# Two cross attentions re-ordered: a head pipeline carried across key blocks, paired score matmuls, an earlier block count

## Chip, cores and metric

One Trainium2 chip, one of its cores. The metric is the device time of one execution, in microseconds (us); the median of the runs shown counts. Engines are named as in the profile: PE is TensorE (PEld its weight loads), DVE is VectorE, ACT is ScalarE, POOL is GpSimd, SP is SyncE, which issues all the DMAs here.

## The reference, cut to what matters

Two layers act on x (256 tokens x 256): a cross attention, a self attention and a feed-forward part each. The change touches the two cross attentions only. ctx is 4096 x 192; the mask leaves out the same trailing keys for every query.

```python
# layer 0: 16 heads of 64, masked
q = xn @ Wq;  k, v = split(ctx @ Wkv)            # Wkv 192 x 2048
out = softmax(where(mask, q k^T / 8, -inf)) v    # per head
x = x + out @ Wo + bo
# layer 1: one head of 256, no mask
q, k, v = xn Wq + bq, ctx Wk + bk, ctx Wv + bv
x = x + softmax(q k^T) v
```

Everything is float32. The profile counts each float32 matmul as two instructions.

## The kernel before

`build` writes one program per engine; the order within an engine is the order of the code, and semaphores tie the engines together. Tokens are two tiles of 128 (t = 0, 1).

**Ahead of the loop.** SP loads x, the identity, the mask, Wq and Wkv (L393 to L403). DVE normalizes x (`layer_norm`), PE turns it (`turn_xn`), ACT scales it into xnT (L976). DVE finds in `find_blocks` which of the eight 512-key blocks hold a key (L1191, L1194). PE projects q with 32 matmul instructions (L471) and counts the blocks between the first 8 and the other 24 (L478). `find_range` on DVE (L1201 to L1210) makes `first` and `n_blocks` from the count, and signals `range_set`. SP then loads both into registers and issues the DMAs of the first block (`load_block`, L409 and L411). PE makes keys and values of head pairs 0 and 1 (`keys_and_values`, L492 to L497: four matmuls of 512 columns, of which the two with 64 rows lie in different halves of the array), and only then does the loop start.

**First attention.** The loop runs over `n_blocks` blocks (two here), and in it over head pairs p = 0 to 7, each with two tiles t. Per pair and tile:

- PE `scores(p, t)`, L527: two heads, 64 rows each, into banks 2s and 2s+1 of slot s.
- DVE `maxima`, L1245 to L1253: adds the mask in place, takes the negated maxima, and the running ones.
- ACT `exps`, L1002: `prob`, and `alpha` = exp(old maximum - new one), L1006.
- PE `turn`, L538: eight transposes of `prob` into banks 4 (head e = 0) and 5 (e = 1).
- ACT copies bank 4 to `probT` (`copy_pT`, L1014), DVE copies bank 5 (L1259).
- Per pair, PE `values(p)`: transposes alpha (L546) and multiplies probT with the values (L553). DVE `add_values` (L1264, L1267) scales `o_acc` and adds.

PE's order in a step p is scores(p, 0), turn(p-1, 1), values(p-2), scores(p, 1), turn(p, 0), keys_and_values(p+2). Pairs 6 and 7 have no keys_and_values left. After pair 7 the block ends with keys_and_values(0) for the next block, values(6), turn(7, 1), keys_and_values(1) for the next block, values(7); the last block does these too, for a block that does not exist. The slots for scores and for keys and values are the same four banks 0 to 3. SP loads the next block when keys_and_values(7) is done.

**After the loop.** DVE inverts the sums l (L1293, L1295). PE spreads 1/l over 64 partitions per head with 64 matmul instructions against the identity (L584). DVE scales `o_acc` pair by two (L1300), PE projects with Wo (L594, 32 instructions). The next stages follow (L602 on).

**Second attention.** 8 units u: 1024 keys and one tile each, UNITS = 8, t = u % 2. Before it PE makes q4 (L804) and its product with Wk and bk (`qk_a` with 128 rows, `qk_b` with 65: 64 channels and the bias, against a row of ones in `ctxT_b`; L810). Per unit PE does `scores4` (L825 with 128 rows, L826 with 65, for two halves of 512 keys), `turn4(u-1)` (L836), `values4(u-2)` (L847). DVE finds the maxima (L1544, L1547), copies one half of p4T, and adds; ACT does the exponentials (L1125) and copies the other half (L1135).

Of the kernel before, what the change touches and what calls it, by code (L numbers as in the profile page):

```python
# [63 lines left out]
def build(nc, a, out):  # L64
    with ExitStack() as ctx:
# [50 lines left out]
        alpha = region_u[:, 5248:7296].rearrange("p (m t e d) -> p m t e d", m=XP, t=TT, e=2)  # L116
        region_d = sb("region_d", [P, 8192])
# [68 lines left out]
        ctxT_b = region_d[0:CD - P + 1, S2:2 * S2]  # L186
# [3 lines left out]
        qk_b = part(region_g, 768, T)[0:CD - P + 1]  # L190
# [6 lines left out]
        nm4_run = sb("nm4_run", [P, TT])  # L197
        nm4_new = sb("nm4_new", [P, TT])
# [66 lines left out]
        l_scaled, run_kept = sem("l_scaled"), sem("run_kept")  # L265
        l_ready, recip_psum = sem("l_ready"), sem("recip_psum")
# [112 lines left out]

        def keep_first(act, nth, banks):  # L380
# [11 lines left out]
        def _(sp):  # L392
# [13 lines left out]
            n_blocks = sp.value_load(rng_i[0:1, 1:2], min_val=1, max_val=NBLK)  # L406
# [7 lines left out]
            load_block(within(first, NBLK - 1))  # L414
            sp.dma_start(rows[:, :], a["rows"].partition_broadcast(P)).then_inc(rows_in, 16)
# [26 lines left out]
            sp.dma_start(ctxT_b[0:CD - P], a["ctxT"][P:CD, 0:S2]).then_inc(ctxT_in, 16)  # L442
# [19 lines left out]
        def _(pe):  # L462
            pe.wait_ge(ident_in, 16)
            pe.wait_ge(consts_set, 2)
            turn_xn(pe, 1, (bank[0], bank[1]))
            pe.wait_ge(weights_in, 16)
            pe.wait_ge(xnT_ready, 2)
            for m in range(8):
# [6 lines left out]
                if m == 1:  # L475
                    pe.wait_ge(blocks_seen, 1)
                    for t in range(TT):
                        mm = nc.tensor.matmul(bank[2][0:1, 0:NBLK], lhsT=ones[:, 0:1], rhs=seen[:, t, :],  # L478
                                              start=t == 0, stop=t == TT - 1)
                    mm.then_inc(blocks_counted, 1)  # L480

            def slot_of(p, t):

                return t if p == XP - 1 else (p + t) % 2

            def keys_and_values(p):

                own, s = slice(p * P, (p + 1) * P), p % 2
# [13 lines left out]
            pe.wait_ge(ctx_landed, 48)  # L502
# [5 lines left out]
            pe.wait_ge(q_ready, 4)  # L508
            with pe.Fori(0, n_blocks) as i:
# [5 lines left out]
                def scores(p, t):  # L515
                    s = slot_of(p, t)
                    pe.wait_ge(k_ready, base8 + (p + 1))
                    if p == XP - 1:
                        pe.wait_ge(prob_ready, base32 + (4 * (p - 1) + 2 * t + 2))
                    elif t == 1 or p == 0:  # L520
                        pe.wait_ge(k_ready, base8 + (p + t + 1))
                        pe.wait_ge(v_ready, base8 + (p + t + 1))
                    else:
                        pe.wait_ge(prob_ready, base32 + 4 * p)
# [6 lines left out]
                def turn(p, t):  # L531
                    u = 2 * p + t
                    for e in range(2):
                        pe.wait_ge(prob_ready, base32 + (2 * u + e + 1))
                        if u >= 1:
                            pe.wait_ge((pT_even, pT_odd)[e], base16 + u)
                        for k in range(KT_PER):
                            mm = nc.tensor.transpose(bank[4 + e][:, k * P:(k + 1) * P],  # L538
                                                     prob[:, u % 2, e, k * P:(k + 1) * P], ident[:, :])
                        mm.then_inc(pT_psum, 1)  # L540

                def values(p):
                    pe.wait_ge(o_added, base8 + (p + 1))
                    pe.wait_ge(alpha_ready, base16 + (2 * p + 2))
                    for t in range(TT):
# [1221 lines left out]
```

## Time and profile before

| | us |
|---|---|
| three runs | 519.38, 523.21, 525.88 |
| median | 523.21 |
| the profiled execution, its own time | 523.5 |
| its span (first to last instruction) | 521.7 |
| busy: PE | 465.3 |
| busy: DVE | 286.6 |
| busy: ACT | 171.2 |

The profile is that of the third line. Its span is 1.8 us shorter than that execution's time. Times in the rows count from the start of the span. A busy time is a union: two matmuls that run side by side count once.

### The profile page before, as it was taken

Reading aid. Unit: us, or ns where it says so; the run is one execution under the profiler, and the core shown is the slowest. Engines: PE = TensorE matmul, PEld = TensorE weight load, DVE = VectorE, ACT = ScalarE, POOL = GpSimd, SP = SyncE. Lnnn points to the kernel's source line nnn. Section 1 sums busy time; section 2 is a strip of 40 time slices with the busy share of each in tenths; the row PEclk is TensorE's granted clock in tenths of the full one; section 3 lists DMA queues with packets and bytes.
Section 4 is the critical chain, followed back from the end, with each engine's and each line's share of the span. In section 5 each row is a group of like instructions: output and inputs, shape, how many; then the busy total and the mean of one; then the engine's idle time right before and its main releaser. Section 6 shows DMA issues by size and latency. Waiting matters only on the chain.

```text
span 521.7 us, 8539 instructions
## 1 busy us (share of the span) xinstructions
PE 465.3 (89%) x3199; PEld 325.7 (62%) x3199; DVE 286.6 (55%) x925; ACT 171.2 (33%) x428; POOL 4.1 (1%) x6
## 2 busy tenths in 40 slices
PE   3888999878999889977769989989979999889997
PEld 2534554443545459874456878878855668767774
DVE  5155777455767644457746997960045444445332
ACT  1154555434555511364731232000013233124110
POOL 0000000000000000000000002000000000000000
PEclk9898999889999999998888999659999999989999
DMA  8300001000002910800004945600048000000000
GB/s 293 105 2 1 1 0 42 1 0 0 0 0 61 363 64 1 322 2 1 1 1 142 336 143 188 136 0 0 1 132 318 1 1 0 1 0 2 0 1 21
DMA packets 21469, 35.02 MB, mean 67 GB/s; under 512 B 1663, under 2 KB 18048, under 8 KB 20864
## 3 DMA queue, kind: packets, MB, share of 16 engines
q1 hardware_dynamic: 21440, 34.64, 20.5%
q8 instruction: 18, 0.29, 0.2%
q14 instruction: 11, 0.09, 0.1%
HBM read 34.37 MB, written 0.26 MB: 66 GB/s over the span
## 4 chain that ended last, share of the span: by engine, by line
PE 73%; DVE 16%; issue 5%; ACT 2%; DMA 1%; DVEq 0%; SPq 0%; POOL 0%; ACTq 0%
PE bank L553 6%; PE bank L538 6%; PE bank L793 6%; PE bank L931 5%; PE bank L527 4%; PE bank L495 4%; PE bank L847 3%; PE bank L492 3%; PE bank L493 3%; PE bank L825 3%; PE bank L826 3%; PE bank L783 2%; PE bank L471 2%; PE bank L945 1%; DMA region_a<-in_Wq 1%
## 5 line engine op out<-in xcount | busy, mean ns | idle before, releaser
L1002 ACT ACTIVATE region_g<-bank,nm_new 128x512 f32<-128x512 f32 x64 | 43.4, 683 | 59.8 <-DVE nm_new L1250 59.8
L538 PEld LDWEIGHTS bank<-ident,region_g 128*128 128x128 f32 x256 | 28.8, 145 | 36.3 <-ACT region_d L1014 24.4
L538 PE MATMUL bank<-ident,region_g 128*128 128x128 f32 x256 | 36.9, 289 | 12.1 <-ACT region_d L1014 7.4
L1245 DVE CUSTOM_DVE_ANT_0 bank<-bank,bias_h 128x512 f32<-128x512 f32 x64 | 43.0, 713 | 4.5 <-issue 4.5
L527 PE MATMUL bank<-region_a,qT 64*128 64x512 f32 x128 | 34.6, 619 | 0.0
L1221 DVE COPY region_a<-bank 128x512 f32<-128x512 f32 x18 | 12.5, 692 | 38.3 <-PE bank L497 38.3
L553 PE MATMUL bank<-region_d,region_a 128*64 128x256 f32 x256 | 32.8, 400 | 0.0
L793 PE MATMUL bank<-region_u,region_g 128*128 128x256 f32 x128 | 29.6, 396 | 1.5 <-issue 1.5
L318 ACT ACTIVATE root<-var 128x2 f32<-128x2 f32 x6 | 1.2, 203 | 87.7 <-DVE var L328 87.7
L783 PE MATMUL bank<-region_a 64*128 64x32 bf16 x768 | 27.3, 249 | 2.4 <-DVE region_a L1499 1.8
L793 PEld LDWEIGHTS bank<-region_u,region_g 128*128 128x128 f32 x128 | 25.5, 200 | 5.3 <-issue 1.6
L783 PEld LDWEIGHTS bank<-region_a 64*128 64x128 bf16 x768 | 26.2, 153 | 3.8 <-DVE region_a L1499 2.6
L762 PE MATMUL bank<-xnT,region_d 128*128 128x256 f32 x128 | 28.0, 379 | 0.0
L762 PEld LDWEIGHTS bank<-xnT,region_d 128*128 128x128 f32 x128 | 24.3, 190 | 3.7 <-issue 0.5
L931 PE MATMUL bank<-xnT,region_u 128*128 128x256 f32 (+1 forms) x112 | 25.6, 384 | 0.0
L1259 DVE COPY region_d<-bank 128x512 f32<-128x512 f32 x32 | 22.1, 692 | 5.7 <-PE bank L538 5.4
L553 PEld LDWEIGHTS bank<-region_d,region_a 128*64 128x64 f32 x256 | 17.5, 141 | 10.3 <-issue 3.6
L323 DVE BATCH_NORM_STATS2 bn<-bank 128x6 f32<-128x256 f32 x8 | 3.0, 422 | 37.8 <-PE bank L793 29.7
L931 PEld LDWEIGHTS bank<-xnT,region_u 128*128 128x128 f32 (+1 forms) x112 | 20.4, 186 | 4.6 <-issue 1.7
L492 PE MATMUL bank<-ctx_a,region_a 128*128 128x512 f32 x36 | 20.7, 661 | 2.0 <-issue 2.0
L847 PE MATMUL bank<-region_a,region_g 128*128 128x192 f32 x128 | 22.0, 326 | 0.0
L1125 ACT ACTIVATE region_g<-bank,nm_new 128x512 f32<-128x512 f32 x16 | 10.9, 683 | 33.8 <-DVE nm_new L1547 33.8
(299 smaller groups left out, 833.9 us busy)
## 6 DMA issues: line engine op xcount, KB each, us to landing
region_d<-in_downT SPq DMA_DIRECT2D x2, 2048.0 KB, 10.6
region_u<-in_up SPq DMA_DIRECT2D x2, 2048.0 KB, 11.9
region_a<-in_ctx SPq DMA_DIRECT2D x1, 3072.0 KB, 16.5
region_d<-in_w_q SPq DMA_DIRECT2D x1, 2048.0 KB, 12.3
region_d<-in_ctxT SPq DMA_DIRECT2D x1, 2048.0 KB, 11.5
region_u<-in_wg SPq DMA_DIRECT2D x1, 1728.0 KB, 7.8
region_u<-in_wu SPq DMA_DIRECT2D x1, 1728.0 KB, 11.7
region_a<-in_wd SPq DMA_DIRECT2D x1, 1664.0 KB, 15.9
```

What stands on the lines that cost most here:

```text
L492: nc.tensor.matmul(bank[2 * s][:, :], lhsT=wkv[:, 0, own], rhs=ctx_a[:, :], start=True, stop=False)
L527: mm = nc.tensor.matmul(bank[2 * s + e][:, :], lhsT=qT[own, p, t * P:(t + 1) * P], rhs=keys[own, p, :], start=True, stop=True)
L538: mm = nc.tensor.transpose(bank[4 + e][:, k * P:(k + 1) * P], prob[:, u % 2, e, k * P:(k + 1) * P], ident[:, :])
L553: mm = nc.tensor.matmul(bank[6 + p % 2][64 * e:64 * e + 64, 0:T], lhsT=v_blk[:, k, (2 * p + e) * XD:(2 * p + e + 1) * XD], rhs=probT[:, p ...
L762: mm = nc.tensor.matmul(bank[(6, 7, 0, 1)[b % 4]][:, (e % 2) * T:(e % 2 + 1) * T], lhsT=downT[:, c, e * P:(e + 1) * P], rhs=xnT[:, c, :], ...
L783: mm = nc.tensor.matmul(bank[2 + 2 * g + t][:, :].rearrange("p (h s) -> p h s", h=ET)[:, :, s], lhsT=hot_lo[own, g, :, s], rhs=hot_hi[own, ...
L793: mm = nc.tensor.matmul(bank[6 + t][:, 0:D], lhsT=hidden[:, e, t * P:(t + 1) * P], rhs=up[:, e, :], start=False, stop=e == ET - 1)
L847: mm = nc.tensor.matmul(bank[6 + u % 2][:, 0:CD], lhsT=p4T[:, u % 2, k * P:(k + 1) * P], rhs=ctx_rows[:, i * 8 + k, :], start=k == 0, stop ...
L931: mm = nc.tensor.matmul(bank[b][0:size, at:at + T], lhsT=w[:, c, m * P:m * P + size], rhs=xnT[:, c, :], start=c == 0, stop=c == DC - 1)
L1002: nc.scalar.activation(prob[:, u % 2, e, :], bank[2 * s + e][:, :], ACT.Exp, scale=-1.0, bias=nm_new[:, p, t, e:e + 1], accum_out=l_blk[:, ...
L1245: ins = nc.vector.tensor_tensor_reduce(bank[2 * s + e][:, :], bank[2 * s + e][:, :], bias_h[:, t, :], -1.0, 3e38, ALU.add, ALU.min, accum_ ...
L1259: nc.vector.tensor_copy(probT[:, p % 2, 1, :, t * P:(t + 1) * P], bank[5][:, :].rearrange("p (k q) -> p k q", k=KT_PER)).then_inc(pT_odd, 1)
```

## The change

1. **Count first.** On PE, 14 transposes of the identity into bank 3 (nothing reads them) and the block count stand ahead of the q projection. SP loads only `first` before the first block's DMAs; `n_blocks` and a new 128 KB load, `pick_pair`, come after them.
2. **Pipeline across blocks.** keys_and_values(0) and (1) move into the loop's start; values(6), turn(7, 1) and values(7) of a block run in the first steps of the next one, and after the loop for the last block. In the first block these slots work on zeroed buffers: four memsets on POOL at the start (prob 1024 elements a partition, alpha 512, probT 4096, v_blk 1024). No keys or values are made for a block that does not exist.
3. **Order and engines within.** For tiles t = 1 ACT copies both halves of probT (`turned_half`), ahead of exps(p+1, 0) but behind exps(7, 0) in step 7; for t = 0 ACT copies head e = 0 and DVE head e = 1, as before. In step 7, values(5) stands ahead of turn(6, 1). The sums l are added per pair in DVE's loop (`add_sums`) and no longer once a block.
4. **1/l.** Two transposes of `l_rep` and eight matmuls with 32 rows (`pick_pair`) in place of the 64 instructions; `scale_output` works per pair, pair 7 after values(7).
5. **Second attention.** The bias term leaves `qk_b`: its 64 rows are stored once per tile at partitions 64t, `ctxT_b` is loaded twice (two DMAs of 1 MB), and the 64-row matmuls of t = 0 and t = 1 follow each other for the same half. The bias is a column `q_bk4` (8 one-column instructions); `maxima4` adds one small DVE instruction, `shift4`. Two units form an iteration: turn4 and the 128-row scores of each tile, the four 64-row matmuls, then both values4.

The core of the diff (SP's, POOL's and allocation lines are told above):

```diff
             turn_xn(pe, 1, (bank[0], bank[1]))
+            for k in range(14):
+                nc.tensor.transpose(bank[3][:, k % 4 * P:(k % 4 + 1) * P], ident[:, :], ident[:, :])
+            pe.wait_ge(blocks_seen, 1)
...
+                pe.wait_ge(ctx_landed, base48 + 48)
+                keys_and_values(0)
+                turn(-1, 1, base16, base32)
+                keys_and_values(1)
                 for p in range(XP):
                     scores(p, 0)
+                    if p == XP - 1:
+                        values(p - 2, base8, base16)
                     if p >= 1:
-                        turn(p - 1, 1)
-                    if p >= 2:
-                        values(p - 2)
+                        turn(p - 1, 1, base16, base32)
+                    if p < XP - 1:
+                        values(p - 2, base8, base16)
                     scores(p, 1)
-                    turn(p, 0)
+                    turn(p, 0, base16, base32)
                     if p + 2 < XP:
-                        pe.wait_ge(prob_ready, base32 + (4 * p + 2))
                         keys_and_values(p + 2)
-                pe.wait_ge(ctx_landed, base48 + 96)
-                pe.wait_ge(prob_ready, base32 + 30)
-                keys_and_values(0)
-                values(XP - 2)
-                turn(XP - 1, 1)
-                pe.wait_ge(prob_ready, base32 + 32)
-                keys_and_values(1)
-                values(XP - 1)
-
+            values(-2, n_blocks * 8, n_blocks * 16)
+            turn(-1, 1, n_blocks * 16, n_blocks * 32)
             pe.wait_ge(l_ready, 1)
...
+            values(-1, n_blocks * 8, n_blocks * 16)
             pe.wait_ge(wo_in, 16)
...
+            for i in range(1, UNITS // TT + 1):
+                for t in range(TT):
+                    turn4(TT * (i - 1) + t)
+                    if i < UNITS // TT:
+                        scores4_a(i, t)
+                if i < UNITS // TT:
+                    for half in range(2):
+                        for t in range(TT):
+                            mm = scores4_b(i, half, t)
+                            if half == 1:
+                                mm.then_inc(s4_psum, 1)
+                for t in range(TT):
+                    values4(TT * (i - 1) + t)
...
+                copy_keys(0)
+                for e in range(2):
+                    turned_half(-1, 1, e, base32)
+                copy_keys(1)
                 for p in range(XP):
-                    exps(p, 0)
+                    if p == XP - 1:
+                        exps(p, 0)
                     if p >= 1:
-                        copy_pT(p - 1, 1)
+                        for e in range(2):
+                            turned_half(p - 1, 1, e, base32)
+                    if p < XP - 1:
+                        exps(p, 0)
                     exps(p, 1)
-                    copy_pT(p, 0)
+                    turned_half(p, 0, 0, base32)
```

## Rows read from the trace of the kernel before

**Rows 1.** Windows: length, busy us (instructions) of PE, PEld, DVE, ACT, POOL, granted clock, DMA, GB/s.
```profile
22.30:110.70 88.40, 82.62 (x418) 40.99 (x418) 51.61 (x156) 42.29 (x108) 0.00 (x0) 0.94 0.03 8
110.70:189.90 79.20, 72.81 (x402) 37.95 (x400) 51.17 (x156) 39.84 (x105) 0.00 (x0) 0.98 0.24 80
189.90:202.60 12.70, 10.86 (x100) 9.90 (x99) 4.84 (x11) 0.00 (x0) 0.00 (x0) 1.00 0.01 1
...
390.40:436.00 45.60, 45.59 (x192) 30.12 (x193) 20.70 (x58) 13.88 (x42) 0.00 (x0) 1.00 0.27 99
...
48.00:84.00 36.00, 36.00 (x204) 18.74 (x204) 25.11 (x77) 19.34 (x53) 0.00 (x0) 1.00 0.00 1
```

**Rows 2.** Timeline of PE, one step of the first attention: start, length, engine, instruction.
```profile
133.12 1.13 PE L527 MATMUL bank<-region_a,qT 64*128 64x512 f32 x4
134.18 1.09 PE L538 MATMUL bank<-ident,region_g 128*128 128x128 f32 x8
135.11 1.02 PE L492 MATMUL bank<-ctx_a,region_a 128*128 128x512 f32 x2
...
137.89 1.03 PE L527 MATMUL bank<-region_a,qT 64*128 64x512 f32 x4
...
140.09 1.95 PE L553 MATMUL bank<-region_d,region_a 128*64 128x256 f32 x16
141.96 1.13 PE L527 MATMUL bank<-region_a,qT 64*128 64x512 f32 x4
```

**Rows 3.** Timeline of PE around the loop's seams and behind it, with idle time before.
```profile
42.87 1.89 PE L538 MATMUL bank<-ident,region_g 128*128 128x128 f32 x8 [1.86 <-ACT region_d L1014]
...
115.35 1.97 PE L538 MATMUL bank<-ident,region_g 128*128 128x128 f32 x8 [2.68 <-ACT region_g L1002]
...
173.56 1.09 PE L538 MATMUL bank<-ident,region_g 128*128 128x128 f32 x8 [1.86 <-ACT region_d L1014]
...
195.38 7.17 PE L594 MATMUL bank<-wo,region_g 128*128 128x256 f32 x32
```

**Rows 4.** Timeline ahead of the loop, PE and SP's queue.
```profile
10.18 3.78 PE L471 MATMUL bank<-xnT,region_a 128*128 128x256 f32 x8 [2.68 <-DMA region_a<-in_Wq]
...
14.07 6.23 PE L471 MATMUL bank<-xnT,region_a 128*128 128x256 f32 x24
...
17.12 0.36 SPq L409 DMA_DIRECT2D ctx_a<-in_ctxT  x1
...
22.30 1.83 PE L492 MATMUL bank<-ctx_a,region_a 128*128 128x512 f32 x2 [1.99 <-issue]
```

**Rows 5.** Groups by line over the whole span: busy us, mean ns, idle before.
```profile
L1014 ACT COPY region_d<-bank 128x512 f32<-128x512 f32 x32 | 18.6, 581 | 4.5 <-PE bank L538 4.5
...
L355 PE MATMUL bank<-ident 128*128 128x128 f32 x104 | 13.3, 289 | 0.0
...
L584 PE MATMUL bank<-ident,l_blk 128*64 128x128 f32 x64 | 3.7, 274 | 1.8 <-DVE l_blk L1295 1.8
...
L635 PE MATMUL bank<-region_a 32*128 32x256 f32 x64 | 4.6, 400 | 1.0 <-DVE region_g L1359 1.0
...
L826 PE MATMUL bank<-region_d,region_g 65*128 65x512 f32 x32 | 16.4, 592 | 0.0
```

**Rows 6.** Timeline of ACT in the step of rows 2.
```profile
140.68 0.69 ACT L1002 ACTIVATE region_g<-bank,nm_new 128x512 f32<-128x512 f32 x1 [1.99 <-DVE nm_new L1250]
```

**Rows 7.** Timeline of the second attention: one unit of PE, and its last.
```profile
412.07 1.02 PE L825 MATMUL bank<-region_d,region_g 128*128 128x512 f32 x2
...
418.99 1.02 PE L825 MATMUL bank<-region_d,region_g 128*128 128x512 f32 x2
...
429.61 1.29 DVE L1544 TENSOR_REDUCE nm_half<-bank 128x1 f32<-128x512 f32 x2 [2.77 <-PE bank L826]
...
441.17 5.37 PE L847 MATMUL bank<-region_a,region_g 128*128 128x192 f32 x32
```

**Rows 8.** POOL's one large fill (groups by line), and DVE at the start (timeline).
```profile
L1693 POOL MEMSET region_d<- 1x4096 f32 x1 | 3.6, 3556 | 88.9 <-PE bank L762 88.9
...
4.62 0.17 DVE L328 TENSOR_SCALAR var<-mv 128x2 f32<-128x2 f32 x1
```

More of the change, by code:

```diff
@@ L474, in _ @@
                     mm.then_inc(q_psum, 1)
[L475 to L484, printed above, removed]
             def keys_and_values(p):
-                own, s = slice(p * P, (p + 1) * P), p % 2
+                own, s = slice(p * P, (p + 1) * P), slot_of("kv", p)
                 half, k = p // KT_PER, p % KT_PER
@@ L589, in _ @@
+            for j in range(2):
+                for g in range(4):
+                    own = slice(32 * g, 32 * g + 32)
+                    mm = nc.tensor.matmul(bank[g][:, j * T:(j + 1) * T], lhsT=pick_pair[own, j, :], rhs=l_T[own, :],
+                                          start=True, stop=True)
+            mm.then_inc(recip_psum, 1)
+            values(-1, n_blocks * 8, n_blocks * 16)
             pe.wait_ge(wo_in, 16)
             for c in range(8):
-                if c % 2 == 0:
-                    pe.wait_ge(oT_ready, c // 2 + 1)
+                pe.wait_ge(oT_ready, c + 1)
@@ L807, in _ @@
             pe.wait_ge(q4_ready, 2)
-            for m, rows_m in ((0, P), (1, CD - P + 1)):
+            for c in range(DC):
+                mm = nc.tensor.matmul(bank[3][:, 0:T], lhsT=wk4T[:, c, 0:P], rhs=q4T[:, c, :],
+                                      start=c == 0, stop=c == DC - 1)
+            mm.then_inc(qk4_psum, 1)
+            for c in range(DC):
+                for t in range(TT):
+                    mm = nc.tensor.matmul(bank[4][64 * t:64 * t + 64, 0:P], lhsT=wk4T[:, c, P:CD],
+                                          rhs=q4T[:, c, t * P:(t + 1) * P], start=c == 0, stop=c == DC - 1)
@@ L809, in _ @@
+            mm.then_inc(qk4_psum, 1)
+            for t in range(TT):
                 for c in range(DC):
-                    mm = nc.tensor.matmul(bank[3 + m][0:rows_m, 0:T], lhsT=wk4T[:, c, m * P:m * P + rows_m],
-                                          rhs=q4T[:, c, :], start=c == 0, stop=c == DC - 1)
-                mm.then_inc(qk4_psum, 1)
-            pe.wait_ge(ctxT_in, 32)
+                    mm = nc.tensor.matmul(bank[5][:, t:t + 1], lhsT=q4T[:, c, t * P:(t + 1) * P],
+                                          rhs=wk4T[:, c, CD:CD + 1], start=c == 0, stop=c == DC - 1)
@@ new lines, in scores4_a, with scores4_b @@
+            def scores4_a(i, t):
+                if i >= 1:
+                    pe.wait_ge(p4_ready, 2 * (TT * (i - 1) + t + 1))
+                for half in range(2):
+                    nc.tensor.matmul(bank[2 * t + half][:, :], lhsT=qk_a[:, t * P:(t + 1) * P],
+                                     rhs=ctxT_a[:, keys4(i, half)], start=True, stop=False)
+            def scores4_b(i, half, t):
+                own = slice(64 * t, 64 * t + 64)
+                return nc.tensor.matmul(bank[2 * t + half][:, :], lhsT=qk_b[own, :], rhs=ctxT_b[own, keys4(i, half)],
+                                        start=False, stop=True)
@@ L1303, in _ @@
+            dve.wait_ge(o_added, n_blocks * XP + 3)
+            for p in range(XP - 1):
+                scale_output(p)
+            add_values(-1, n_blocks * 8)
+            dve.wait_ge(o_added, n_blocks * XP + 4)
+            scale_output(XP - 1)
             dve.wait_ge(rows_in, 16)
```

304 lines of the change are left out of this document (161 added, 143 removed).

## The prediction

> **What bounds the kernel now.** I read the windows by stage first. In the two blocks of the first attention PE is busy 82.6 of 88.4 us and 72.8 of 79.2 us, DVE and ACT never over two thirds; in the second attention PE is busy throughout [rows 1]. So both stages are PE's, and time comes only from PE's work, its idle time or its clock. Then PE's timeline: a full step of the first attention lasts 8.84 us (133.12 to 141.96), of which keys_and_values is 2.78 (135.11 to 137.89); without it a step is 6.06 [rows 2]. From 48 to 84 us nothing but such steps runs, at clock 1.00 and with no gap [rows 1]. A block's work is therefore 6 x 8.84 + 2 x 6.06 + 2 x 2.78 = 70.7 us, and two blocks are 141.4.
>
> Last the seams. PE starts the first keys at 22.30 [rows 4] and the Wo projection at 195.38 [rows 3]: 173.1 us. Work explains 141.4 + 2 x 2.78 (keys made ahead of the loop, while the last block makes two pairs for nobody) + 3.7 for 1/l [rows 5] = 150.7. The other 22.4 us are idle time and low clock. Of these (1 - 0.94) x 88.4 + (1 - 0.98) x 79.2 = 6.9 us are clock [rows 1]: after the waits at 42.87 and 115.35 eight transposes take 1.89 and 1.97 us, where they take 1.09 otherwise [rows 3, 2], so PE falls to its level of 1.2 GHz behind the holes. The holes are the fill of each block's pipeline (PE waits for the first maxima and exponentials: 1.86 and 2.68 us before those rows alone) and pair 7, where turn(6, 1) waits 1.86 us for the copy of turn(6, 0), which ACT makes only after exps(6, 1) [rows 3].
>
> **The change part by part.** All times are in the profiled execution (523.5 us, span 521.7), which lies 0.3 above the median of the three runs.
>
> *Front.* Before, the count waits behind 8 projection instructions that take 3.78 us, 0.47 each, against 0.26 for the following 24 [rows 4]: PE is at its low level there by these durations. Now 28 transpose instructions run ahead of it, from about 7.5 us on, behind the turned xn. They cost 0.128 each [rows 5], 3.6 us, at full clock and twice that at half: they end between 11.1 and 14.7. I take 12.0, since PE no longer rests before Wq lands and should rise midway. The count ends at 12.2 instead of 14.07, where the 24 start; the projection's 32 instructions at 0.22 end at 19.4, and the last copy of q (0.6) and the loop's entry (some 0.5) allow keys_and_values(0) at 20.5. The first block's data: before, SP issued at 17.12, 3.0 us behind the count, with two registers loaded; one register less saves about 0.8, so issue at 14.4, and with the same 5.2 us from issue to first use [rows 4] it is there at 19.6. PE decides: 20.5 against 22.30, a gain of 1.8. Bounds: -0.7 (transposes all slow) and +2.8 (all fast). `pick_pair` stands behind the block's DMAs and is used 150 us later: nothing.
>
> A rule speaks against this part. The row: a POOL fill of 4096 elements takes 3.56 us, 0.87 ns an element, and DVE's little tensor_scalar on SBUF runs at 4.62 us [rows 8]. No run here shows the two engines together on such operations. The Trainium skill, "SBUF — State Buffer", section "Who interferes with whom", says that a DVE tensor_scalar in a two-port mode and a GpSimd instruction block each other for the whole instruction. By it DVE would wait at 4.62 for the fill of probT; its price is with the rivals. By the trace alone the four fills (6656 elements, 5.8 us) end near 6.5 and cover nothing that waits before 20 us.
>
> *Loop.* Each block keeps its 70.7 us: the slots of values(6), turn(7, 1), values(7) move to the next block's start and hold the same number of instructions. In the first block they work on zeros. What waits change? In a full step exps(p, 0) starts 2.79 us after its scores (140.68 against 137.89) [rows 6, 2]. Now ACT first copies both halves of turn(p-1, 1), which PE ends 2.2 us after those scores: two copies of 0.58 [rows 5] end at about 2.8, so the exponentials start as before, and turn(p, 0), due 5.1 us after the scores, has 1.6 us in hand. ACT then works 3.3 + 1.7 + 0.6 = 5.6 of 8.84 us. Behind exps on ACT's queue stand copies for turn(p, 1), due later than before. In step 7 values(5) (2.2 us) fills the 1.86 us wait; next late is turn(7, 0), which needs bank 4 and 5 free: ACT reaches these copies after exps(7, 0), about 0.45 us after PE is ready. Two blocks: 0.9. At the seam PE goes from turn(7, 0) to keys_and_values(0) (its data has been loading for 12 us), turn(7, 1), keys_and_values(1), scores(0, 0), values(6), scores(0, 1): values(6) covers the first exponentials, keys_and_values(2) the second. In the first block the zero work covers them too, with 0.4 of remaining waits. PE still idles ahead of its first keys, a little shorter: I take half of the 1.5 us by which the low clock stretched them before (7.05 us for two pairs instead of 5.56), 0.8.
>
> *Behind the loop.* From the end of turn(7, 0): values(6) 2.2, turn(7, 1) to 3.1; DVE adds pair 6, the sums, inverts and spreads l, to 4.7; two transposes 0.45, DVE's copy 0.42, eight 32-row matmuls (16 instructions at 0.072 [rows 5] are 1.2) to 7.1; values(7) to 9.3. The Wo projection starts at 9.3, and pair 7 is scaled long before its turn in it.
>
> Sum for this stretch: 141.4 + 0.9 + 0.4 + 0.8 + 9.3 = 152.8 instead of 173.1, gain 20.3. It is the two pairs of keys (5.6), the 1/l matmuls (3.7 to 1.7), minus the zero work (5.3), plus 22.4 - 4.4 = 18.0 of holes and slow clock. Bounds: if ACT's new duties cost 0.7 us in each of 12 full steps, 12; if clock and waits go altogether, 23. Then Wo's 7.1 us and all to 384 us are shifted and unchanged; the 8 us of loads behind the last block start 28 us before their use now, and still some 22 after.
>
> *Second attention.* A unit lasts 6.92 us (412.07 to 418.99) [rows 7]; its 65-row scores are 4 of 32 instructions in 16.4 us [rows 5], 2.05 by busy time, 1.72 by the starts. Two units cost 13.84. Two 64-row matmuls side by side cost 1.06 for four instructions (L527 [rows 2]), or 0.96 between other work, so eight cost 1.9 to 2.1 in place of 3.44: an iteration of two units is 12.4, gain 1.4, three times: 4.3. At the other end they don't overlap and the gain is 0. What is late: both tiles' maxima are now ready together. DVE needs 1.29 for a reduction [rows 7], some 2.1 with its small instructions, so the second tile's exponentials end 5.6 us after the scores; PE fills 5.2 with values4, 0.9 with turn4 and 1.7 with scores before it needs them. It holds. In the first iteration there are no values to fill: 0.5 lost; the bias instructions before the first scores cost 0.2 beyond what the copies hide. Last values end at 442.8 instead of 446.5 [rows 7]: gain 3.7, bounds -0.6 and 4.6.
>
> Sum: 523.5 - 1.8 - 20.3 - 3.7 = 497.7 us.
>
> **Rivals.**
> (a) ACT is late in every full step, since its three copies stand between exponentials; for it, the chain above leaves only 0.1 us between the second copy and the maxima; against it, 1.6 us in hand at turn(p, 0). At 0.7 us x 12 more: 506.
> (b) The paired scores don't shorten the second attention (two accumulating matmuls into different banks do not overlap, or DVE's two maxima in a row hold PE): 501.4. For it: no row shows pairs that add to a bank begun by a 128-row matmul except L495 and L497, which do overlap. That speaks against it.
> (c) DVE waits at 4.62 for the probT fill, which runs from about 1.8 to 5.4, so 0.8 us, and the chain to the first keys moves with it: 498.5. This is the result of the rule above.
> (d) All holes go and the first matmuls are fast: 493.
> (e) Slower. PE's clock: if the work without holes ran at 1.2 GHz for longer than 36 us of the 141, the low clock would eat the 25.8 us and 10.5 more. Say it held for the first block: 70.7 us more, 568. From 48 to 84 us the same work ran at 1.00 [rows 1], against it.
> (f) The zero work delays the first block rather than fill it, because the slots follow each other in PE's order: 2.2 to 5.3 us, so up to 503.
>
> **Chances.** Forecast 0.48 (its own range 494 to 501), (a) 0.12, (b) 0.13, (c) 0.09, (d) 0.06, (e) 0.03, (f) 0.09. About 2% (10.5 us) is what a measurement of this kernel can tell from no change, so the line is 512.7: all but (e) and the worst of (a) with (b) lie below it. Faster 0.90, same 0.07, slower 0.03. Range 492 to 508: to (d) below and past (a) above.
>
> **What would show it.** Right: keys_and_values 32 times in L492's group, not 36; no PE wait over 1 us between the first keys and the end of the loop, except behind the first projection; block 1's first turn follows keys_and_values(0) at once; first keys near 20.5 us; the Wo projection near 173 us; the 64-row scores of the second attention at about 1 us for four. Wrong: idle PE before turn(p, 0) with ACT as releaser (a); 0.86 us between starts of every two 64-row scores (b); DVE idle near 4.6 us (c); clock under 0.9 in the loop (e). The forecast fails as a whole if the first stretch stays over 160 us.

## The result, and the profile after

| | before | after |
|---|---|---|
| median of all runs (range), us | 523.33 (519.38 to 525.88) | 498.21 (496.66 to 504.54) |
| ratio, 95% interval | | 0.9553 (0.9494 to 0.9611) |
| the profiled execution: time, span | 523.5, 521.7 | 498.52, 496.7 |

The change makes the kernel 4.5% faster by the ratio; the medians lie 25.1 us (4.8%) apart, where 25.8 us was forecast. Ratios and their intervals leave out executions that a lower granted clock set back, here the one of 504.54 us. In the profiled executions, by the starts of the same work:

| stretch of PE | before | after | gain | forecast |
|---|---|---|---|---|
| start to the first keys | 22.30 | 19.68 | 2.6 | 1.8 |
| first keys to the Wo projection | 173.1 | 151.5 | 21.5 | 20.3 |
| Wo to q4 (unchanged code) | 189.5 | 189.7 | -0.2 | 0 |
| q4 to the end of the last values | 61.7 | 59.0 | 2.7 | 3.7 |
| the rest (unchanged code) | 75.2 | 76.8 | -1.7 | 0 |

Windows over the last four of these stretches, after (columns as in rows 1):

```profile
19.68:171.20 151.52, 149.88 (x862) 78.21 (x862) 99.20 (x340) 91.33 (x229) 0.00 (x0) 1.00 0.14 47
171.20:360.91 189.71, 167.17 (x1681) 140.61 (x1680) 114.45 (x408) 49.64 (x123) 0.39 (x1) 0.90 0.31 94
360.91:419.88 58.97, 57.57 (x285) 40.15 (x286) 29.20 (x83) 18.62 (x50) 0.00 (x0) 1.00 0.28 98
419.88:496.70 76.82, 69.39 (x328) 52.27 (x327) 31.46 (x98) 16.64 (x34) 0.00 (x0) 0.95 0.01 4
```

In the first attention PE is busy for all but 1.6 us, and its granted clock is 1.00; before it was 0.94 and 0.98 [rows 1]. In the last row the clock is 0.95; before it was 0.97 there. That is the only difference that the unchanged end shows, and the end is 1.7 us longer.

Before, PE waited six times for `prob` or `probT` between the first keys and Wo, three of them in rows 3. PE's waits there, before:

```profile
PE bank L538 <- ACT region_d L1014: 7.4, 4, 1.9
PE bank L538 <- ACT region_g L1002: 4.7, 2, 2.7
```

(us in total, times, longest). All six, and the slow transposes behind two of them, are gone from the loop. PE's timeline over pairs 6 and 7 and the seam between the blocks, after (start, length, line; L566 scores, L526 turn, L535 and L543 values, L505 keys):

```profile
78.53 1.02 PE L566 MATMUL bank<-region_a,qT 64*128 64x512 f32 x4
...
85.74 0.44 PE L535 MATMUL bank<-ident,region_u 128*128 128x128 f32 x2
86.11 1.95 PE L543 MATMUL bank<-region_d,region_a 128*64 128x256 f32 x16
87.99 1.09 PE L526 MATMUL bank<-ident,region_g 128*128 128x128 f32 x8
89.01 1.13 PE L566 MATMUL bank<-region_a,qT 64*128 64x512 f32 x4
90.07 1.15 PE L526 MATMUL bank<-ident,region_g 128*128 128x128 f32 x8
91.11 1.12 PE L505 MATMUL bank<-ctx_a,region_a 128*128 128x512 f32 x2
```

No line has a bracket, so nothing waited. values(5) at 85.74 fills the place of the old wait, and the next block's keys follow the last turn at once. The waits left around this stretch all stand at its two ends:

```profile
PE bank L505 <- ACT qT L1017: 0.9, 1, 0.9
PE bank L526 <- ACT region_d L1026: 0.8, 1, 0.8
PE bank L600 <- DVE region_u L1346: 0.6, 1, 0.6
PE bank L590 <- DVE region_u L1341: 0.3, 1, 0.3
```

They are the first keys behind the last copy of q, turn(7, 1), and the two steps of 1/l. ACT's new order in a full step (timeline of ACT; L1026 copies for turn(p-1, 1), L1045 exponentials):

```profile
71.33 1.07 ACT L1026 COPY region_d<-bank 128x512 f32<-128x512 f32 x2 [0.85 <-PE bank L526]
72.48 0.69 ACT L1045 ACTIVATE region_g<-bank,nm_new 128x512 f32<-128x512 f32 x1
```

The scores of this step start at 69.69, so the exponentials start 2.79 us behind them, the same distance as in rows 6, and turn(p, 0) at 74.82 finds the first of them done at 73.17: the 1.6 us in hand of the forecast.

The ends. Timeline of PE ahead of the loop (L483 the 14 spare transposes, L486 the count, L494 the projection), then behind it:

```profile
8.12 3.19 PE L483 MATMUL bank<-ident 128*128 128x128 f32 x14
11.24 0.25 PE L486 MATMUL bank<-seen,ones 128*1 128x8 f32 x4
11.42 7.40 PE L494 MATMUL bank<-xnT,region_a 128*128 128x256 f32 x32
19.68 1.12 PE L505 MATMUL bank<-ctx_a,region_a 128*128 128x512 f32 x2 [0.87 <-ACT qT L1017]
```

The 14 spare transposes take 3.12 us, start to start, 0.22 each; in rows 2 eight transposes take 0.93 us, 0.12 each. So PE runs at its low level there by the durations, although the granted clock reads 1.00 in this window. The projection behind them is fast: 0.22 us from instruction to instruction, where the first eight took 0.47 before [rows 4].

```profile
162.48 0.40 PE L535 MATMUL bank<-ident,region_u 128*128 128x128 f32 x2
...
165.52 1.07 PE L526 MATMUL bank<-ident,region_g 128*128 128x128 f32 x8 [0.76 <-ACT region_d L1026]
166.85 0.44 PE L590 MATMUL bank<-ident,region_u 128*128 128x128 f32 x2 [0.27 <-DVE region_u L1341]
167.90 1.15 PE L600 MATMUL bank<-region_u 32*128 32x256 f32 x16 [0.61 <-DVE region_u L1346]
...
171.22 1.13 PE L608 MATMUL bank<-wo,region_g 128*128 128x256 f32 x4
```

From the end of turn(7, 0) to Wo it is 8.74 us, forecast 9.3. The second attention, timeline of PE from its first scores (L848 128 rows, L853 64 rows):

```profile
366.41 1.96 PE L848 MATMUL bank<-region_d,region_g 128*128 128x512 f32 x4
368.30 1.98 PE L853 MATMUL bank<-region_d,region_g 64*128 64x512 f32 x4
370.21 1.98 PE L848 MATMUL bank<-region_d,region_g 128*128 128x512 f32 x4
...
374.04 1.09 PE L862 MATMUL bank<-ident,region_g 128*128 128x128 f32 x8
...
379.91 1.99 PE L853 MATMUL bank<-region_d,region_g 64*128 64x512 f32 x8
381.82 5.47 PE L873 MATMUL bank<-region_a,region_g 128*128 128x192 f32 x32
387.13 1.04 PE L862 MATMUL bank<-ident,region_g 128*128 128x128 f32 x8
...
399.63 0.60 PE L862 MATMUL bank<-ident,region_g 128*128 128x128 f32 x4
```

At 379.91 eight 64-row instructions take 1.91 us, as long as four do at 368.30. An iteration is 12.50 (387.13 to 399.63), forecast 12.4. But the first four groups take 1.91 each (7.63 us from 366.41 to 374.04), where the same number of instructions took 1.72 before (6.96 us, 390.40 to 397.36).

### The profile page after: what moved, and what is told of

It is laid out like the page before. It is cut to its first block, busy times and chain, and to the rows that moved or that the text cites. A ratio compares the mean times of both kernels' runs of the same rounds, so it can differ in the third digit from the quotient of the medians.

```text
span 496.7 us, 8618 instructions
## 1 busy us (share of the span) xinstructions
PE 455.6 (92%) x3207; PEld 321.3 (65%) x3207; DVE 284.8 (57%) x959; ACT 181.1 (36%) x444; POOL 6.4 (1%) x9
## 4 chain that ended last, share of the span: by engine, by line
issue 43%; PE 40%; DVE 15%; POOL 1%; ACT 1%; DVEq 0%; POOLq 0%
PE bank L807 6%; PE bank L968 5%; PE bank L873 4%; PE bank L848 2%; PE bank L797 2%; PE bank L853 2%; PE bank L982 2%; DVE region_a L1400 1%; DVE region_a L1498 1%; PE bank L862 1%; PE bank L382 1%; PE bank L692 1%; PE bank L776 1%; PE bank L986 1%; DVE region_a L1556 1%
## 5 line engine op out<-in xcount | busy, mean ns | idle before, releaser
L1045 ACT ACTIVATE region_g<-bank,nm_new 128x512 f32<-128x512 f32 x64 | 43.4, 682 | 40.8 <-DVE nm_new L1305 40.0
L526 PEld LDWEIGHTS bank<-ident,region_g 128*128 128x128 f32 x264 | 28.2, 141 | 24.8 <-issue 12.1
L526 PE MATMUL bank<-ident,region_g 128*128 128x128 f32 x264 | 36.2, 280 | 0.8 <-ACT region_d L1026 0.8
L543 PE MATMUL bank<-region_d,region_a 128*64 128x256 f32 x288 | 35.1, 385 | 0.0
L566 PE MATMUL bank<-region_a,qT 64*128 64x512 f32 x128 | 34.7, 618 | 0.0
L1026 ACT COPY region_d<-bank 128x512 f32<-128x512 f32 x50 | 27.5, 587 | 11.0 <-PE bank L526 11.0
L1318 DVE COPY region_a<-bank 128x512 f32<-128x512 f32 x16 | 11.1, 692 | 29.4 <-PE bank L510 29.3
L968 PE MATMUL bank<-xnT,region_u 128*128 128x256 f32 (+1 forms) x112 | 27.2, 402 | 0.0
L543 PEld LDWEIGHTS bank<-region_d,region_a 128*64 128x64 f32 x288 | 19.1, 136 | 10.8 <-issue 3.0
L968 PEld LDWEIGHTS bank<-xnT,region_u 128*128 128x128 f32 (+1 forms) x112 | 21.5, 197 | 5.1 <-issue 1.7
L873 PEld LDWEIGHTS bank<-region_a,region_g 128*128 128x128 f32 x128 | 20.7, 190 | 2.3 <-issue 2.3
L1166 ACT ACTIVATE region_g<-bank,shift 128x512 f32<-128x512 f32 x16 | 10.8, 683 | 24.9 <-DVE shift L1608 24.9
## 6 DMA issues: line engine op xcount, KB each, us to landing
region_d<-in_downT SPq DMA_DIRECT2D x2, 2048.0 KB, 10.4
region_d<-in_w_q SPq DMA_DIRECT2D x1, 2048.0 KB, 12.4
```

Of the source, the lines that this page charges most:

```text
L543: mm = nc.tensor.matmul(into[64 * e:64 * e + 64, 0:T], lhsT=v_blk[:, k, (2 * m + e) * XD:(2 * m + e + 1) * XD], rhs=probT[:, m % 2, e, k, ...
L566: mm = nc.tensor.matmul(bank[2 * s + e][:, :], lhsT=qT[own, p, t * P:(t + 1) * P], rhs=keys[own, p, :], start=True, stop=True)
L873: mm = nc.tensor.matmul(bank[6 + u % 2][:, 0:CD], lhsT=p4T[:, u % 2, k * P:(k + 1) * P], rhs=ctx_rows[:, i * 8 + k, :], start=k == 0, stop ...
L968: mm = nc.tensor.matmul(bank[b][0:size, at:at + T], lhsT=w[:, c, m * P:m * P + size], rhs=xnT[:, c, :], start=c == 0, stop=c == DC - 1)
L1026: nc.scalar.copy(probT[:, p % XP % 2, e, :, t * P:(t + 1) * P], bank[4 + e][:, :].rearrange("p (k q) -> p k q", k=KT_PER)).then_inc((pT_ev ...
L1045: nc.scalar.activation(prob[:, u % 2, e, :], bank[2 * s + e][:, :], ACT.Exp, scale=-1.0, bias=nm_new[:, p, t, e:e + 1], accum_out=l_blk[:, ...
```

## The experiments

The edits are to the changed kernel, except in before_step7.

### What fills the wait at pair 7, and what does a wait cost?

turn_first puts the old order of step 7 back into the changed kernel; before_step7 gives the kernel before the new one, and nothing else.

```diff
 turn_first:
-                    if p == XP - 1:
-                        values(p - 2, base8, base16)
                     if p >= 1:
                         turn(p - 1, 1, base16, base32)
-                    if p < XP - 1:
-                        values(p - 2, base8, base16)
+                    values(p - 2, base8, base16)
 before_step7:
+                    if p == XP - 1:
+                        values(p - 2)
                     if p >= 1:
                         turn(p - 1, 1)
-                    if p >= 2:
+                    if 2 <= p < XP - 1:
```

> The changed kernel with step 7 of the first attention in the old order: turn(6, 1) ahead of values(5). Theory (values(5) fills a wait of 1.86 us twice, of which 0.45 came back behind it): PE waits near 1.9 us in each block again, run 2.8 us longer, up to 1.7 more per block if PE's clock falls behind the wait: 501 to 504. Rival (the seam's wait went through the pipeline across blocks): no change, 498.2.

Measured: 502.88 us (500.42 to 509.77), ratio 0.9657 (0.9619 to 0.9694). The unpaired kernel below ran on the same chip and equals the changed one in this stretch; its ratio is 0.9576 (0.9559 to 0.9593), so the old order costs 4.2 us (0.0081 of the 520.05 us before). In the profile, of the execution of 509.77 us, the stretch from the first keys to Wo is 158.0 us instead of 151.5. PE's timeline in the first block:

```profile
88.30 1.89 PE L526 MATMUL bank<-ident,region_g 128*128 128x128 f32 x8 [1.78 <-ACT region_d L1023]
89.98 0.63 PE L535 MATMUL bank<-ident,region_u 128*128 128x128 f32 x2
90.55 2.57 PE L543 MATMUL bank<-region_d,region_a 128*64 128x256 f32 x16
```

and in the second:

```profile
162.97 1.09 PE L526 MATMUL bank<-ident,region_g 128*128 128x128 f32 x8 [1.78 <-ACT region_d L1023]
```

The wait is back in both, 1.78 us each. Behind the first, the same instructions take 1.6 us longer (88.30 to 93.04, granted clock 0.66 from 88 to 93 us, against 3.1 us for the same three groups in the second); behind the second they don't. So each hole here cost its own length, and nearly that length again only where the clock fell. From the scores of pair 7 for t = 0 to those for t = 1, the stretch that the edit touches, the two blocks together are 5.0 us longer than in the changed kernel. The other 1.6 us of the 6.5 lie behind the loop (173.48 to Wo: 4.90 us instead of 3.32), where the edit changes nothing and the clock fell too.

> The kernel before with one edit: in step 7 values(5) stands ahead of turn(6, 1). Theory (the two waits of 1.86 us and the low clock behind one of them are local to step 7): 2.8 to 4.5 us shorter than the kernel before, 519 to 520.5. Rival (without the pipeline across blocks the wait only moves to the block's end): 523.3, as before.

Measured: 512.7 us (509.96 to 518.93), where the kernel before had 520.05 on that chip; ratio 0.9854 (0.98 to 0.9907), which is 4.8 to 10.4 us. From the first keys to Wo 165.2 us instead of 173.1. The waits of PE there:

```profile
PE bank L538 <- ACT region_g L1004: 4.7, 2, 2.7
PE bank L538 <- ACT region_d L1016: 3.7, 2, 1.9
```

Those at L1016 (L1014 before) were four and 7.4 us, so two waits, 3.7 us, went. The rest is clock: four equal windows of this stretch show 0.96, 1.00, 1.00, 1.00 where those of before show 0.92, 0.96, 0.96, 1.00, and the wait of 2.68 us in front of the second block is still there but no longer followed by slow transposes:

```profile
111.09 1.32 PE L538 MATMUL bank<-ident,region_g 128*128 128x128 f32 x8 [2.68 <-ACT region_g L1004]
```

In the kernel before the same wait had them at 1.97 us [rows 3]. Not all of this is the edit's. Where it acts, in pair 7 of the two blocks, two waits of the kernel before are gone, and with them its 1.6 us of slow instructions behind the first:

```profile
94.01 3.53 PE L553 MATMUL bank<-region_d,region_a 128*64 128x256 f32 x16
```

These places are 5.1 us shorter in before_step7 (3.4 in the first block, 1.8 in the second). Of the other 2.8 us, 1.7 lie at the first keys, ahead of the edited code (22.30 to the first scores at 29.77, against 23.12 to 28.94), and 1.1 behind the 2.68 us wait at the seam. And the stretch from Wo to q4, which no edit touches, was 4.3 us shorter in this execution. So the line of order is worth 5.0 to 5.1 us where it acts, by both edits: a fifth of the whole gain. By the ratios, which take in the unchanged stretches, it is 4.2 us in the one direction and 7.6 in the other.

### Has ACT the slack that the forecast gave it?

Two and five extra copies of bank 4 (read by nobody) ahead of exps(p, 0), in the twelve steps p = 1 to 6 of the two blocks. Two take 1.2 us, five take 3.1 us:

```diff
                         for e in range(2):
+                            if e == 0 and p < XP - 1:
+                                act.wait_ge(pT_psum, base32 + (4 * p + 1))
+                                for x in range(N):
+                                    nc.scalar.copy(scratch[:, :], bank[4][:, :]).then_inc(extra, 1)
...
                             turned_half(p - 1, 1, e, base32)
```

> The changed kernel with two further copies of 0.58 us on ACT (bank 4 to a scratch tile, each waited for) ahead of exps(p, 0) in each of the twelve steps p = 1 to 6. Theory (the exponentials are 1.65 us early for turn(p, 0)): a step stays at 8.84 us, the run at 497 to 499. Rival (ACT is at its edge, since its copies stand between the exponentials): 1.3 us more in twelve steps, 514.

> The same with five further copies, some 3.3 us. Theory (only what exceeds 1.65 us shows): 1.6 to 1.9 us more in twelve steps, step 10.5 us, run near 519. Rival (edge): 3.3 us more a step, 538. Rival (DVE or PE covers it some other way): under 505.

Measured: with two, 499.06 us, and the stretch from the first keys to Wo is unchanged at 151.5 us. With five, 517.68 us, and it is 171.1: 19.6 more, 1.63 a step. PE's waits with five:

```profile
PE bank L528 <- ACT region_g L1048: 17.0, 12, 1.4
```

Twelve waits for the exponentials, one in each of these steps, where the kernel as changed has none. With two copies the exponentials start 1.0 us later behind their scores than in the changed kernel (3.83 against 2.79 us), and that costs nothing. With five they start 2.9 us later (5.70), and that costs 1.63: the slack lies near 1.3 us. The forecast's 1.6 was of the right kind, and it is what decides that rival (a) didn't come.

### The front: count, spare transposes, POOL's fills, the wait for q

```diff
 no_spare (count_behind: this, and the count behind the projection's first 8):
-            for k in range(14):
-                nc.tensor.transpose(bank[3][:, k % 4 * P:(k % 4 + 1) * P], ident[:, :], ident[:, :])
 pool_late:
+            pool.wait_ge(range_set, 1)
             nc.gpsimd.memset(prob[:, 1], 0.0).then_inc(prob_ready, 2)
 both_fixes (pool_late, and this):
-            pe.wait_ge(q_ready, 4)
...
                 keys_and_values(0)
+                pe.wait_ge(q_ready, 4)
                 turn(-1, 1, base16, base32)
```

> The changed kernel without the 14 transposes ahead of the count. Theory (they give the projection a fast clock): the projection's first 8 instructions take some 0.47 us each again, range_set comes 0.6 us earlier, but the first keys start near 20.8, 1.1 later than with them. Rival (only the order matters, the transposes are in the way): first keys at 19.7 or earlier.

> The changed kernel with the front undone: no transposes, the count behind the projection's first 8 instructions. Theory (the front's gain is worth 2.6 us): first keys at 22.3 to 22.8 instead of 19.68, run some 2.9 us longer. Rival (the gain comes from loading one register less ahead of the data): first keys near 20.5, run 0.8 longer.

> The changed kernel with POOL's four fills behind range_set. Theory (the two engines block each other): DVE's tensor_scalar at 4.62 takes 0.17 us again instead of 1.00, the first keys start at 18.9 instead of 19.68, 0.8 us off the run. Rival (the long tensor_scalar has another cause, such as the extra DVE fills ahead of it): it stays at 1.0 us and the first keys at 19.7.

> The changed kernel with two edits: POOL's four fills start only behind range_set, and PE waits for the last copy of q behind keys_and_values(0) instead of ahead of the loop. Theory (POOL's fill of probT holds DVE's small tensor_scalar at 4.62 for 0.83 us; behind that the first keys wait 0.87 us for the copy of q): first keys at 18.1 instead of 19.68 us, run 1.6 us shorter than the changed kernel, 496.6. Rival (the data of the first block or the register loads set the first keys): first keys no earlier than 19.5, run as the changed kernel, 498.2.

| kernel | time | first keys | Wo | Wo to q4 |
|---|---|---|---|---|
| changed | 498.52, the profiled execution | 19.7 | 171.2 | 189.7 |
| no_spare | 503.59, one execution | 20.5 | 172.2 | 192.8 |
| count_behind | 502.60, one execution | 21.9 | 173.5 | 190.4 |
| pool_late | 490.96, one execution | 18.8 | 170.3 | 185.1 |
| both_fixes | 499.64 (490.49 to 502.75) | 17.6 | 169.1 | 191.6 |

The starts are one execution each. With the changed front as it is, the first keys start between 19.5 us (after_again, act2) and 20.4 us (turn_first), since the projection takes between 7.17 and 8.10 us. The earlier count is worth 1.4 us (21.9 to 20.5), more than this scatter. The spare transposes are worth 0.8 against the one profile of the changed kernel, and 0.1 to 1.0 against all of these. Without them PE rests 2.41 us ahead of the count, and the projection then takes 8.69 us, longer than in any profile with them:

```profile
10.74 0.25 PE L484 MATMUL bank<-seen,ones 128*1 128x8 f32 x4 [2.41 <-DVE seen L1238]
10.91 8.69 PE L492 MATMUL bank<-xnT,region_a 128*128 128x256 f32 x32
```

Seven of its instructions begin 0.41 to 0.59 us after one another before the 0.22 us comes; in the changed kernel it is one, in turn_first four, in after_again none.

POOL's fills cost DVE 0.83 us at 4.62, rival (c). POOL and DVE in the changed kernel, then DVE with the fills late:

```profile
2.08 3.52 POOL L1755 MEMSET region_d<- 128x4096 f32 x1
...
4.62 1.00 DVE L334 TENSOR_SCALAR var<-mv 128x2 f32<-128x2 f32 x1
```

```profile
4.75 0.17 DVE L334 TENSOR_SCALAR var<-mv 128x2 f32<-128x2 f32 x1
```

The tensor_scalar ends at 5.6, when the fill does (2.08 + 3.52), and is back at the 0.17 us of rows 8 when no fill runs. The trace thus agrees with the Trainium skill, "SBUF — State Buffer", section "Who interferes with whom", by which whichever of the two has the shared port first keeps it for its whole instruction. In act5 the same tensor_scalar began at 4.71 and took 1.80 us: it ended only when the next fill (5.53 to 6.48) did. With both edits PE starts the first keys at 17.6 without a wait, 2.0 earlier, and Wo is 2.1 earlier. So these edits do what they should. In the time they can't be told from scatter: the ratio of both_fixes is 0.9433 (0.935 to 0.9516), which overlaps that of the changed kernel, and the last column varies by more than they are worth, as told below.

### Is it the pairing that shortens the second attention's scores?

```diff
-                    for half in range(2):
-                        for t in range(TT):
+                    for t in range(TT):
+                        for half in range(2):
```

Now four instructions on the same 64 rows stand ahead of the four on the other 64.

> The changed kernel with the four 64-row score matmuls of an iteration of the second attention ordered tile by tile, so that neighbours use the same rows of the array. Theory (the gain there is the overlap of the two tiles): eight instructions take about 3.5 us instead of 1.91, an iteration 14.0 instead of 12.5, three times: 502.8 for the run. Rival (the gain comes from the new order of turns and values, DVE's work hides the rest): iteration under 12.9, run at 498 to 499.

Measured: 497.62 us (496.43 to 498.38), ratio 0.9576 (0.9559 to 0.9593). The iteration (387.11 to 399.62) is 12.51, and its eight instructions take what they took before:

```profile
379.89 1.99 PE L853 MATMUL bank<-region_d,region_g 64*128 64x512 f32 x8
381.81 5.47 PE L873 MATMUL bank<-region_a,region_g 128*128 128x192 f32 x32
```

The order within the eight doesn't matter. In short windows their starts come in twos, near 379.9, 380.4, 380.8 and 381.3, as in the changed kernel. What the gain needs is that rows of both halves stand together in the eight, not that they alternate. Whether PE itself looks that far ahead, or the instructions reached it in another order than written, the trace doesn't say.

### 1/l by 64 matmuls, without the selector

The transposes and the copy ahead of the selector's matmuls go too.

```diff
...
-                        mm = nc.tensor.matmul(bank[g][:, j * T:(j + 1) * T], lhsT=pick_pair[own, j, :], rhs=l_T[own, :],
-                                              start=True, stop=True)
+                        mm = nc.tensor.matmul(bank[p % 4][64 * e:64 * e + 64, at:at + P],
+                                              lhsT=l_rep[:, t, 0, 2 * p + e:2 * p + e + 1].to_broadcast([P, XD]),
+                                              rhs=ident[:, :], start=True, stop=True)
...
```

> The changed kernel with 1/l spread by 64 matmuls against the identity, as before, and no transposes, copy and selector matmuls. Theory (PE works and waits 2.13 us between l_ready and values(7) now, 3.75 with the old matmuls, all of it on the path): Wo's projection starts 1.6 us later than at 171.2. Rival (DVE's scaling is what Wo's projection waits for): 171.2 to 171.6, no change.

Measured: 499.25 us, Wo at 172.8 instead of 171.2. The 64 instructions take 3.71 us:

```profile
166.91 3.71 PE L596 MATMUL bank<-ident,region_u 128*64 128x128 f32 x64 [0.26 <-DVE region_u L1338]
170.55 0.44 PE L535 MATMUL bank<-ident,region_u 128*128 128x128 f32 x2
```

from 166.91 to 170.55 against 166.85 to 168.98 in the changed kernel: the selector is worth 1.5 us.

### Where the scatter comes from

> The changed kernel once more, unedited, as the yardstick for the next kernel on the same chip. Theory (its scatter of several us comes from stretches in which the granted clock falls behind a hole, above all in the unchanged stages between the Wo projection and q4): first keys 19.7, Wo 171 and Wo to the end of the last values as before within 0.3 us wherever the clock is 1.00; the median within 496 to 500 and single runs spread over 3 to 8 us. Rival (the scatter is a difference between chips): single runs of this kernel on one chip agree within 1 us.

> The changed kernel with POOL's fills of probT, prob, alpha and v_blk behind range_set, in place of its start, against the unedited one on the same chip. Theory: DVE no longer waits at 4.6 us, first keys and Wo 0.8 to 0.9 us earlier, and nothing else moves, so the median is 0.9 us lower, which the scatter of either hides; the 7 us lower look of before was clock. Rival (the fills cost more than the one DVE wait, or the earlier start shifts the later stages out of the holes that slow the clock, each time): the median is 4 us lower or more, near 491, and the stretch from Wo to q4 is shorter than 188 us in this profile too.

Measured on one chip: the changed kernel again 498.84 us (491.72 to 503.5), ratio to before 0.9519 (0.9421 to 0.9617); with late fills 495.73 us (492.63 to 503.77), ratio 0.9521 (0.9443 to 0.9599). No difference can be claimed, and the runs of one kernel on this chip spread over 11 us. On the chip of turn_first they did not: seven runs of the kernel before lay within 0.8 us there, where eleven on this one spread over 11. So the chip, or the time of the run, has a part in the scatter. From Wo to q4 it was 191.1 us in the one profile and 186.4 in the other, on code that the edit doesn't touch.

The timeline of PE in this stretch shows why. A step of the self attention begins at L700, after a wait of 1.89 or 1.90 us each time. The changed kernel:

```profile
215.86 0.94 PE L700 MATMUL bank<-region_a 32*128 32x256 f32 x16 [1.90 <-DVE nm L1400]
216.72 1.93 PE L692 MATMUL bank<-region_a,region_g 128*32 128x256 f32 x16
...
225.06 0.94 PE L700 MATMUL bank<-region_a 32*128 32x256 f32 x16 [1.89 <-DVE nm L1400]
225.92 1.07 PE L692 MATMUL bank<-region_a,region_g 128*32 128x256 f32 x16
```

and pool_late:

```profile
215.53 0.94 PE L700 MATMUL bank<-region_a 32*128 32x256 f32 x16 [1.90 <-DVE nm L1400]
...
223.13 0.94 PE L700 MATMUL bank<-region_a 32*128 32x256 f32 x16 [1.89 <-DVE nm L1400]
```

The first step took 9.20 us in the one (windows: granted clock 0.81) and 7.60 in the other (clock 1.00), with the same waits. The next step of the changed kernel, behind the same wait, took 7.60 as well (225.06 to 232.66). So the same hole lowers the clock one time and not the next, and here it cost 1.6 us when it did. Eight instructions at L382 took 3.78 us in the changed kernel, at clock 0.50, and 1.99 in pool_late, at 1.00. Over the profiles of all kernels this unchanged stretch lasted from 185.1 us (pool_late) and 185.2 (before_step7) to 192.8 (turn_first, no_spare); with late fills it was 185.1, 186.4 and, in both_fixes, 191.6, so they don't make it short. What decides whether a given hole lowers the clock wasn't found. Nor did pool_late's gain at the front hold in pool_late_again: the count was again 0.7 us earlier, but the projection took 7.97 us instead of 7.17. Its first four instructions stand 0.59, 0.43 and 0.43 us apart, then they come every 0.22: PE left its low level later there, though the granted clock reads 1.00 throughout. Why later stays open.

## Why the prediction was right

**What bounds the kernel** held: both attentions are PE's, and the time came from PE's work, holes and clock. The signs that the prediction named came out but for the 64-row scores at their start. Keys and values run 32 times at L505, no wait inside the loop exceeds 1 us, block 1's keys follow the last turn at once, the first keys start at 19.7 (20.5 forecast), and Wo at 171.2 (173).

**Front: gain 2.6, forecast 1.8.** The size is near, but one term came out by luck. The forecast took the spare transposes as 28 instructions of 0.128 us, 3.6 us at full clock. They are 14: the profile counts a float32 transpose once and only other matmuls twice (a turn of eight is x8 in rows 2). At the 0.12 us of rows 2 they would take 1.6 us. They took 3.19, since all ran at the low level: half the number at half the pace. The forecast's rise of the clock midway through them came only at their end. The count ended at 11.4, not 12.2, and that outweighed the 0.8 us that DVE lost to POOL. SP's issue followed 2.7 us behind the start of the count instead of 3.2, so one register less saved 0.6 us, forecast 0.8. The parts by one profile each are 1.4 for the place of the count and 0.8 for the spare transposes (count_behind, no_spare). The other 0.4 (22.3 to 21.9) has no run of its own and is within the scatter: before_step7, with the old front, started its first keys at 23.1.

**Loop and behind it: gain 21.5, forecast 20.3.** The largest term was right in kind and nearly in size. To the end of turn(7, 0) of the second block it took 142.8 us, forecast 143.5; behind it 8.7, forecast 9.3. Two of the steps were wrong and cancelled. The forecast gave 2.1 us to leftover waits and slow clock, and there were none. A block took 71.4 us and not 70.7, without any wait: the stretch from the scores of pair 6 to the next keys (78.53 to 91.11) is 12.58 us where two steps of 6.06 are 12.12, and the first keys behind a turn take 2.97 instead of 2.78. The figure of 6.06 came from subtracting keys_and_values from a full step, and didn't hold where other instructions become neighbours.

What the gain is made of can be added up from the windows of 22.30 to 195.38 before and 19.68 to 171.20 after: PE's idle time went from 14.0 to 1.6 us, the low clock was worth 6.9, and the selector 1.5, in all 20.8 of the 21.5. The keys no longer made for nobody and the zero work nearly cancel, 5.6 against 5.3 us by the forecast. Runs of their own have only the order of step 7 (5.0) and the selector (1.5). That the other 15 us are the pipeline across the blocks is argued from the waits that are gone, and no run undoes it alone.

**Second attention: gain 2.7, forecast 3.7.** Here the sum failed by 1.0, in two terms. About half is the time ahead of the first turn. The forecast had 0.2 more than before there; the first scores take 7.63 us instead of 6.96, where groups of four instructions with 128 and 64 rows alternate and take 1.91 each instead of 1.72. The bias instructions cost nothing (q4 to the first scores 5.50 us, before 5.53). The other part is the iterations: 13.1, 12.5, 12.5 for a forecast of 12.9, 12.4, 12.4.

**Unchanged stretches: 0 forecast, -1.9 found.** This is the clock. Before_step7 and pool_late show that it could as well have been +4, so that the total lies within 1 us of the forecast is partly luck.

**The rivals.** (a) fell to ACT's slack of about 1.3 us, shown by two and five extra copies. (b) fell: eight paired instructions take as long as four. The reason given for it, that the matmuls are adjacent, was too narrow (unpaired). (c) came true as a mechanism: 0.83 us on DVE, forecast 0.8. It was hidden in the sum by the earlier count. (d) came true for the loop, where no hole was left; the rest of its 493 was missing. (e) fell: clock 1.00 throughout the loop. (f) fell: the first block, with its zero work, takes 71.4 us from keys to keys, as the second does (91.11 to 162.48).

The prediction told the order of step 7 as two waits of 1.86 us filled; with the clock behind the first of them it brings 5 us.

## What to carry to other kernels

Where PE sets the time, price a hole in its stream at its length and, if rows show slow instructions behind it, at up to that length again. Fill it with independent work that is there already: one line that moved values(5) ahead of a turn was worth 5 us. Before judging an edit of a few microseconds by a median, compare the unchanged stretches of the two profiles: here they differ by up to 7.7 us from execution to execution, and only the starts at the edited place tell what the edit did. Do so in more than one profile where you can: even the first 20 us of the same code differ by up to 0.9 us.

## What the runs showed of the hardware that was not expected

- The same wait of 1.9 us on PE was followed by the low clock one time and not the next, for 1.6 us (step 9.20 against 7.60 us).
- At the start of the kernel 14 transposes took 3.19 us, twice what rows 2 give for as many, while the granted clock read 1.00. The projection behind them began 0.22 us apart at once in some executions and after up to four instructions 0.43 us apart in others.
- Four 512-column matmul instructions took 1.91 us, start to start, where groups of 128 and 64 rows alternate, and 1.72 where 128 and 65 rows alternated (before).
- Eight 64-row matmuls on two halves of the array take 1.91 us in either order, alternating or grouped by half.
- A DVE tensor_scalar of two elements a partition stood for 0.83 us behind a POOL fill that had begun 2.5 us earlier, and in act5 for 1.63 us behind two fills in a row.
